# An opening with more identity turns and an earlier weight load, and a last SwiGLU step shared with GpSimd

## The reference: what is computed

```python
c_q = hidden_states @ w_q_down                        # 1024 x 192
q_nope = (c_q @ w_q_up_nope)                          # 32 heads x 128
q_rope = (c_q @ w_q_up_rope)                          # 32 heads x 64, then turned by rope
c_kv, k_rope = hidden_states @ w_kv_down, hidden_states @ w_k_rope
q_lat = einsum('bhsd,hdr->bhsr', q_nope, wuk)
scores = einsum(q_lat, c_kv) + einsum(q_rope, k_rope) # causal, softmax, times c_kv, w_uv, w_out
...
nx = x * rsqrt(mean(x * x) + eps) * ln_w              # 1024 x 512
g = einsum('bsh,ih->bsi', nx, gate_w)                 # 512 -> 1792
u = einsum('bsh,ih->bsi', nx, up_w)
y = einsum('bsi,hi->bsh', silu(g) * u, down_w)        # 1792 -> 512
x = layernorm(x + y)
```

## Time and profile before

| | |
|---|---|
| time, median of 3 runs | 1491.78 us (1489.8 to 1492.79) |
| the profiled execution's own time | 1495.79 us |
| its span, first to last instruction | 1493.9 us |
| TensorE busy | 1428.8 us, 96% of the span, 8098 matmuls |
| VectorE busy | 936.7 us, 63% |
| ScalarE busy | 812.0 us, 54% |
| GpSimd busy | 530.4 us, 36% |
| mean granted clock of TensorE | 0.986 |

### The profile page before, as it was taken

How to read it: one execution, slowest core, us unless ns; L and a number is a source line. 1 busy time by engine, 2 the same in 40 slices (tenths; PEclk the granted TensorE clock), 3 DMA queues, 4 the chain that set the end, 5 groups by cost and what they waited for, 6 DMA issues and landing times. The chain is left out here.

```text
span 1493.9 us, 24032 instructions
## 1 busy us (share of the span) xinstructions
PE 1428.8 (96%) x8098; PEld 1016.8 (68%) x8098; DVE 936.7 (63%) x1526; ACT 812.0 (54%) x1730; POOL 530.4 (36%) x491
## 2 busy tenths in 40 slices
PE   8899999999999999999978988999999999999996
PEld 6676677677677767667656865555555568888885
DVE  4455556555566555556687647766666437777967
ACT  4565676666666666566543323555655666333433
POOL 1433454433344543344040153414140024454542
PEclk9999999999999999999999998999999999999998
DMA  6323333433333443333310044615244042000000
GB/s 222 57 34 52 41 41 49 54 36 48 43 43 45 53 45 41 50 32 41 85 57 1 0 60 68 97 25 77 34 70 124 2 157 83 1 1 0 8 22 29
DMA packets 61763, 75.75 MB, mean 51 GB/s; under 512 B 20609, under 2 KB 42113, under 8 KB 60801
## 3 DMA queue, kind: packets, MB, share of 16 engines
q1 hardware_dynamic: 57344, 64.38, 24.8%
q0 software_dynamic: 4352, 10.49, 5.0%
HBM read 42.58 MB, written 2.10 MB: 30 GB/s over the span
## 5 line engine op out<-in xcount | busy, mean ns | idle before, releaser
L1762 ACT ACTIVATE l_probs<-l_banks 128x512 f32<-128x512 f32 (+3 forms) x366 | 165.8, 495 | 136.9 <-PE l_banks L1706 91.2
L1802 DVE TENSOR_REDUCE pm<-l_sm 128x2 f32<-128x1024 f32 (+1 forms) x192 | 178.3, 956 | 93.6 <-PE l_sm L1676 60.9
L791 ACT ACTIVATE probs<-sc,nmax 128x128 f32<-128x128 f32 (+7 forms) x256 | 190.2, 743 | 71.8 <-DVE nmax L871 68.4
L871 DVE TENSOR_REDUCE nmax<-sc 128x1 f32<-128x128 f32 (+7 forms) x256 | 193.4, 755 | 32.0 <-PE sc L622 26.4
L799 ACT COPY pt<-tb 128x512 f32<-128x512 f32 (+3 forms) x256 | 129.3, 505 | 150.8 <-PE tb L636 150.0
L636 PE MATMUL tb<-ident,probs 128*128 128x128 f32 x1152 | 172.4, 275 | 3.5 <-ACT pt L799 1.9
L78 PE MATMUL sc<-k_h,q_h 128*128 128x512 f32 (+4 forms) x384 | 144.0, 375 | 3.2 <-ACT probs L791 2.3
L636 PEld LDWEIGHTS tb<-ident,probs 128*128 128x128 f32 x1152 | 132.0, 141 | 15.1 <-DVE pt L879 4.4
L1703 PE MATMUL l_banks<-qk_bufs 128*128 128x512 f32 (+3 forms) x366 | 135.8, 413 | 2.4 <-DMA qk_bufs<-mT 2.0
L658 PE MATMUL mb<-pt,ckv 128*64 128x512 f32 (+2 forms) x736 | 131.7, 493 | 3.2 <-DVE x_tok L861 2.9
L78 PE MATMUL sc<-k_h,q_l 128*128 128x512 f32 (+4 forms) x384 | 131.9, 344 | 0.0
(11 more groups left out here) (315 smaller groups left out, 3109.6 us busy)
## 6 DMA issues: line engine op xcount, KB each, us to landing
gated_late<-in_gated SPq DMA_DIRECT2D x11, 768.0 KB, 13.8
wout<-in_w_out SPq DMA_DIRECT2D x16, 512.0 KB, 4.5
rb<-rT SPq DMA_DIRECT2D x248, 32.0 KB, 4.5
late<-late SPq DMA_DIRECT2D x120, 64.0 KB, 2.0
qk_bufs<-late SPq DMA_DIRECT2D x96, 64.0 KB, 5.3
qk_bufs<-late POOLq DMA_DIRECT2D x96, 64.0 KB, 5.9
nope_t<-in_nope_by_dim SPq DMA_DIRECT2D x16, 192.0 KB, 3.9
late<-in_gated SPq DMA_DIRECT2D x3, 768.0 KB, 9.1
```

What stands on the lines that cost most here:

```text
L791: act.activation(prob_row(n, s), score_row(n)[0], ACT.Exp, bias=nmax[:, s:s + 1], accum_out=ssum[:, n:n + 1]).then_inc(exped, 1)
L871: dve.tensor_reduce(nmax[:, n % 4:n % 4 + 1], row, axes, ALU.max, negate=True).then_inc(negmax, 1)
L1762: act.activation(probs[(NC * g + c) % RING][:, h, 0:w], e_slot(g, n)[:, 0:w], ACT.Exp).then_inc(exped, 1)
L1802: dve.tensor_reduce(pm[g % 2][:, :, s, i, half], slot(("m", g, n))[:, :, 0:w], AX.X, ALU.max, negate=True).then_inc(freed, 1)
```

## The change

Five edits. In the opening, 36 identity turns stand in the place of 16. SyncE issues the four loads of pair 1 in the opening, once pair 0's latent products are done, ahead of the copies of the keys (it was the first work of the next stage, behind the split of pair 0's weights). The eight turns of the latent rows stand behind `queries(1)`, and ScalarE's copy of them behind its last `q_h`.

In the SwiGLU, the down products of step 25 move from step 26 to step 27, where they stand behind the gate and up products and ahead of the down products of step 26. In step 27 GpSimd adds the 1 to the four exponentials and makes the four remainders `a_l`; VectorE did both.

```diff
@@ stage_latent, sync
                 sp.dma_start(keep.x[:], ...).then_inc(keep.x_in, 16)
+                sp.wait_ge(sig.wlat_ps, 1)
+                pairs.load_q(sp, 1)
                 for n in range(2):
@@ stage_latent, tensor
                 pe.wait_ge(const_ok, 5)
-                for i in range(16):
+                for i in range(36):
                     pe.transpose(pj[i % 2][:, 0:P], keep.ident[:], keep.ident[:])
...
                 queries(0)
+                queries(1)
                 pe.wait_ge(act_ev, 6)
                 for j in range(ST):
                     last = pe.transpose(pc[:, j, :], k_f[0:KVL, j * P:(j + 1) * P], keep.ident[0:KVL, 0:KVL])
                 last.then_inc(ckv_ps, 1)
-                queries(1)
@@ stage_latent, scalar
                 nope_part(0)
-                act.wait_ge(ckv_ps, 1)
-                act.copy(keep.ckv[:], pc[:])
                 high_query(0, act_ev)
                 nope_part(1)
                 high_query(1, sig.qh_ok)
+                act.wait_ge(ckv_ps, 1)
+                act.copy(keep.ckv[:], pc[:])
@@ stage_mla, sync
-                load_q(-1, 0, 0)
                 steps(0, 0)
@@ stage_gated, tensor, step(n)
                     hidden(n, 1)
-                    if n >= 1:
+                    if 1 <= n < LAST - 1:
                         down_part(n - 1)
+                    if n == LAST:
+                        down_part(LAST - 2)
+                        down_part(LAST - 1)
@@ stage_gated, gpsimd
-                for n in range(STEPS):
-                    if n < LAST:
-                        lower_gu(n + 1)
+                for n in range(LAST):
+                    lower_gu(n + 1)
                     lower_d(n)
+                for j in range(4):
+                    pool.wait_ge(ex_ok, LAST + j + 1)
+                    pool.tensor_scalar(den[:, token_tile(j)], ex[:, token_tile(j)], 1.0, None, ALU.add).then_inc(den_ok, 1)
+                lower_d(LAST)
+                for j in range(4):
+                    cols, u = token_tile(j), LAST % 2
+                    pool.wait_ge(ah_ok, LAST + j + 1)
+                    pool.tensor_tensor(a_l[u][:, cols], act_f[:, cols], a_h[u][:, cols].bitcast(F32),
+                                       ALU.subtract).then_inc(al_ok, 1)
@@ stage_gated, vector
                 def last_silu(j):
                     cols = token_tile(j)
-                    dve.wait_ge(ex_ok, LAST + j + 1)
-                    dve.tensor_scalar(den[:, cols], ex[:, cols], 1.0, None, ALU.add).then_inc(den_ok, 1)
                     dve.wait_ge(den_ok, LAST + j + 1)
...
-                last_lower(0)
                 last_silu(3)
                 last_up(2)
-                last_lower(1)
                 last_up(3)
-                last_lower(2)
-                last_lower(3)
```

More of the change, by code:

```diff
@@ L2311, in last_up @@
                     dve.tensor_tensor(act_f[:, cols], pu[LAST % 2][:, cols], act_f[:, cols], ALU.mult).then_inc(af_ok, 1)
[L2313 to L2317, removed]
                 def last_stats(t):
```

## The result

| | kernel before | changed kernel |
|---|---|---|
| median (range), us, of 3 runs before and 8 of the changed kernel | 1491.78 (1489.8 to 1492.79) | 1485.18 (1480.18 to 1486.83) |
| beside each other, median of 8 runs each, us | 1492.66 | 1485.18 |
| ratio, 95% interval | 1 | 0.9943 [0.993, 0.9956] |
| profiled execution: own time / span | 1495.79 / 1493.9 | 1485.66 / 1483.9 |
| first rise of the clock, at | 14.74 | 6.58 |

By the ratio the kernel became 0.57% faster, by the medians 0.50%; 1483.7 against 1491.78 would be 0.9946. The two profiled spans differ by 10.0, more than the medians' 7.5, because the execution profiled before took 3.1 more than its kernel's 1492.66, and the changed kernel's only 0.5 more than its 1485.18.

What follows compares the result with a forecast made beforehand. TensorE, busy nearly throughout, was taken to bound the kernel, with gains where it is slow or waits, at the two ends. 2.85 + 0.45 + 3.0 + 1.85 = 8.15; 1491.78 - 8.1 = 1483.7 us, overall range 1481.0 to 1488.3.

Steps and rivals of the forecast that it cites:

- The opening: Opening: 36 turns raise TensorE's clock by about 7.9, so project(0) ends at 17.1 instead of 19.87; -2.85 us.
- the bound: Opening: even a clock rise at once gives no more than 2.9 us, since 8.76 is set by `xT_l`.
- The first rival: Opening: the turns don't count for the clock, which gives 0 with the order's term; 1487.0 us, 12 in 100.
- The turned order: End of the first stage: queries 1 start earlier, so TensorE closes the stage at 41.93 instead of VectorE at 42.38; -0.45 us.
- Pair 1's load: Round 0: no wait for `wuk` and the clock holds, so the first query product comes at 49.2, not 52.23; -3.0 us.
- The second rival: Round 0: the clock falls all the same, leaving pair 1's load worth 1.3 to 2; 1485.2 us, 15 in 100.
- The rope chain moves as a whole: Round 0: SyncE's and GpSimd's rope work follows the first query product, so ScalarE's wait at 70.75 gives nothing back.
- The last step: SwiGLU's end: exponentials start 1.8 sooner, then ScalarE becomes last; first residual sum at 1479.6 instead of 1481.47; -1.85 us.
- The third rival: Last step: ScalarE's table load and casts wait for products, 1 us later than reckoned, leaving 0.8; 1484.8 us, 6 in 100.
- lower bound of -2.4: Last step: step 26's down products end at 1478.1, so the gain is no more than 2.4 us.
- The slower rival: Front of layer 1: two more stretches at the lower clock take 10.2 us; 1493.9 us, 3 in 100.
- The sum: Whole kernel: 2.85 + 0.45 + 3.0 + 1.85 = 8.15 us off; from the median, 1483.7 us.

Runs made afterwards that it cites:

- turns36: The kernel before with 36 identity turns in the opening in the place of 16, nothing else; ratio 0.9978.
- swiglu: The kernel before with only the SwiGLU edits: step 25's down products in step 27, GpSimd's added ones and remainders; ratio 0.9988.
- load: The kernel before with only pair 1's load moved into the opening (16 turns, old order); ratio 0.9987.
- again: The changed kernel once more, unaltered, on another chip visit; ratio to the kernel before 0.9953.
- best: both with step 25's and 26's down products laid between step 27's products, and VectorE's third inverse ahead of its first up product; ratio 0.9928.
- bestfill: best with eight identity turns added, four behind the second and four behind the fifth score row of round 0; ratio 0.9922.
- both: The changed kernel with ScalarE's table load ahead of the waiting copy, and round 0's rope transfers elsewhere in SyncE's order; ratio 0.995.
- noturn: The changed kernel with 16 identity turns in the opening in the place of 36; ratio to the kernel before 0.9959.
- order: The kernel before with only queries(1) ahead of the latent turns and ScalarE's copy of them last; ratio 0.9999.
- pool: The kernel before with only GpSimd's added ones and remainders in the last step; one run, last exponential to residual sum 14.82 us, before 17.06.
- down: The kernel before with only step 25's down products moved to step 27; one run, last exponential to residual sum 16.51 us, before 17.06.

## Why the prediction was right, and where it was off

- **The opening, -2.85: -2.64 in the profile, -2.67 in *turns36*.** The mechanism was as written. `project(0)` ended at 17.23 where I had 17.1, since its products took 8.40 and not 8.27, and 17.1 against 19.87 would itself have been 2.77. The rise at 7.9 that I took was the latest of the six; the earlier ones gave nothing more, because the first remainder sets the start of `project(0)`, as the bound had it.
- **The turns count.** The first rival, 1487.0, fell with *turns36*: six rises under 36 turns, none later than 7.94. In *swiglu* and *load* the clock rose at 5.4 and 5.9, when TensorE had run nothing but the 16 turns. Part 4 of "TensorE: Matmul & The Clock Gate" in the Trainium skill, by which the upper clock level doesn't engage in transpose mode because this work doesn't count as TensorE being busy in the same way, isn't borne out for these fp32 turns; the traces print them as MATMUL and don't show the mode. The prediction said that the 16 turns did not raise the clock. In two of the seven traces with 16 turns they did, and it was lost for 3.4 as `project(0)` began; in both TensorE had stood still for 3.2 behind the turns. Behind 36 turns it stood still for 1.3 at most, and the clock was not lost in any of six traces. That the shorter pause is what keeps it fits these eight traces but wasn't tested by itself.
- **The turned order, -0.45: -0.42** in the trace, below what the time shows.
- **Pair 1's load, -3.0: -3.12 in the changed kernel, -1.24 alone.** The size came out, in part by luck. Piece by piece, behind the first score: the first latent product comes 1.42 sooner (1.26 of it the wait), ScalarE's copy another 0.81, the split 0.02, and the query product behind it 0.88; the sum had 1.26, 0.9, 0 and 0.8.

  But wait and clock are two things. With the load in the opening the clock held up to the query product in four traces (changed, *again*, *best*, *bestfill*), fell for 3.4 in two (*both*, *noturn*) and for 6.8 in *load*. With the load in its old place it fell in all six, for 3.4 in *turns36* and *swiglu* and for 6.8 in the others. Between traces with a fall of the same length the load is worth the wait and little more: 1.24 at 6.8 (9.37 against 8.13), 1.5 at 3.4 (8.33 and 8.28 against 6.78). The rest of the 3.12 is there only where the clock holds.

  The prediction had the clock fall in the pause for the load. It did in *before*, *order* and *pool*; in *down* it fell at 44.48, 0.33 ahead of the pause, in *turns36* and *swiglu* over 1 us behind its end, and in *load* without one. So the pause as the cause isn't shown, and what decides between holding and falling is open.

  The second rival's condition does occur in this kernel. I gave it 1.0 to 1.7; a fall of 3.4 cost 0.53 (6.78 against 6.25), the long one in *load* 1.88 (8.13 against 6.25). Neither costs its half; for one thing, ScalarE's and GpSimd's split takes 2.80 to 2.82 in all thirteen traces, whatever the clock does.
- **The rope chain moves as a whole:** it did, but for its scatter of 6.2 to 7.9. ScalarE's wait at `q_h` was 2.62 where I expected 3.8 to stay.
- **The last step, -1.85: -1.85,** in four traces (changed, *again*, *swiglu*, *noturn*: 15.21 or 15.22). Put on the changed kernel's clock (8.19 sooner, the shift of `a_h` of step 26), the working has ScalarE's first cast at 1469.8, TensorE's last products at 1470.46 and the residual sum at 1471.4; measured are 1469.49, 1470.46 and 1471.43. `a_l` took 1.71 for four, so 0.43 each, as estimated. The third rival's queue was in the sum at its right size. What failed is an attribution, which step is worth what: I booked 2.75 of relief on TensorE and asked only what would come last next, not what the step would be without the moved products. It would be 0.39 shorter, as *pool* shows, because these products hold ScalarE's queue: taking the table load out from behind them gave 0.41 back in *both*. My lower bound of -2.4 held for this order of the products alone; *best*, with another, has -3.45.
- **The slower rival** did not come: 32.1 us at the lower clock in the changed kernel's trace, 44.3 in before's (behind the first rise in both).
- **The sum, 8.15.** As measured by the traces the terms are 2.67 + 0.42 + 3.12 + 1.85 = 8.06. The medians differ by 7.5 and the ratio says 8.5, with an interval of 6.6 to 10.4 (0.44 to 0.70% of 1492.66). The time alone doesn't single out the forecast: 1485.18 is 1.5 above its 1483.7 and lies on the second rival's 1485.2 and near the third's 1484.8. In the measurement side by side the kernel before took 0.9 more than its 1491.78, which moves all three up by as much and the forecast to 1484.6. What decides is the traces: in both of the changed kernel the clock held up to the query product, and its casts came where the sum had them.

## What to carry to other kernels

Before booking a product that is moved out of the way as a gain, look for who waits for its end in another engine's queue: here the later products held a buffer, and a table load and four casts stood behind the copy that waited for it. Try such edits one by one, since two that gain 0.55 and 2.24 alone gave 1.85 together, and lay the moved work between the last products rather than ahead of them. A clock that is late in an opening can be won by work that fills the wait ahead of the first real product (2.6 to 2.7 here), while one that falls where another engine's chain is the bound cost only 0.53 of 3.4 and 1.88 of 6.8. And where the clock scatters between executions of the same code, read several traces before a gain is put down to an edit.

## What the runs showed of the hardware

- fp32 identity turns raised the granted clock from 1.2 to 2.4 GHz, with no other work on TensorE: at 4.98 to 7.94 us in six traces with 36 turns from 1.97 on. When exactly, and where it falls later on, differs between executions of the same code: at 767.8 it fell in one trace of the changed kernel and at 69.4 and 755.5 in the other.
- From the same query product to GpSimd's first rope instruction, with DMAs between them, it took 6.2 to 7.9 us over thirteen traces, and 6.2, 7.6 and 7.8 in the three with the same order of SyncE's queue (*both*, *bestfill*, *best*). One trace can't show the worth of a change of that order.
- GpSimd's 128x128 fp32 subtraction took 0.43 us when four ran in a row (1.71), and its addition of a constant 0.58 (2.34 for four in the changed kernel, 2.03 in *pool*).
